# Attention scores of two heads as 64-row tiles of TensorE, units in pairs, in a transformer kernel on one core

## The reference

```python
ada = silu(c) @ W_ada + b_ada                      # shift, scale and gate of both halves
h = modulate(layernorm(x), shift_a, scale_a)
q, k, v = split(h @ W_qkv + b_qkv)                 # 16 heads of 18 channels
scores = einsum('bhqd,bhkd->bhqk', q, k) * 18 ** -0.5
o = einsum('bhqk,bhkd->bhqd', softmax(scores), v)
x = x + gate_a * (o @ W_proj + b_proj)
h = modulate(layernorm(x), shift_m, scale_m)
x = x + gate_m * (gelu(h @ W_up + b_up) @ W_down + b_down)
```

## Time and profile before

| | |
|---|---|
| median of 3 runs | 2154.39 us |
| profiled execution | 2156.56 us, span 2154.9 us |
| mean granted TensorE clock | 0.963 |
| busy, PE / weight loads | 1971.7 / 1748.4 us |
| busy, DVE / ACT / POOL | 1225.6 / 1108.3 / 1028.6 us |
| scores L1683 (768 products) | 244.2 us busy |
| shifted scores L1706 (1536 products) | 245.1 us busy |

### The profile page before, as it was taken

How to read it: one execution, slowest core, us unless ns; L and a number is a source line. 1 busy time by engine, 2 the same in 40 slices (tenths; PEclk the granted TensorE clock), 3 DMA queues, 4 the chain that set the end, 5 groups by cost and what they waited for, 6 DMA issues and landing times. The chain is left out here.

```text
span 2154.9 us, 50055 instructions
## 1 busy us (share of the span) xinstructions
PE 1971.7 (91%) x16599; PEld 1748.4 (81%) x16599; DVE 1225.6 (57%) x2813; ACT 1108.3 (51%) x1909; POOL 1028.6 (48%) x1066
## 2 busy tenths in 40 slices
PE   4684689999999999889999999989989999999996
PEld 2553479998989988778989999888779999898986
DVE  7765465565655556464655646565555556565541
ACT  2222245656465564446565564654555564646552
POOL 2002164454545545564545545445645545454544
PEclk9887689999999999999999999999999999999998
DMA  6604243333233332353333333333433333323320
GB/s 164 159 23 139 81 125 101 98 88 96 81 108 87 97 99 85 92 138 93 84 106 92 93 101 84 98 85 98 111 103 89 98 98 89 94 82 109 88 78 25
DMA packets 139389, 207.65 MB, mean 96 GB/s; under 512 B 35390, under 2 KB 95838, under 8 KB 139006
## 3 DMA queue, kind: packets, MB, share of 16 engines
q1 hardware_dynamic: 110878, 163.54, 27.6%
q10 hardware_dynamic: 24192, 27.94, 4.7%
q0 software_dynamic: 4224, 14.96, 2.4%
HBM read 99.81 MB, written 20.82 MB: 56 GB/s over the span
## 5 line engine op out<-in xcount | busy, mean ns | idle before, releaser
L1928 DVE TENSOR_REDUCE maxima<-scores 128x4 f32<-128x1024 f32 x384 | 461.3, 1224 | 188.5 <-PE scores L1683 183.8
L1259 POOL TENSOR_TENSOR hidden<-g_full,hidden 128x512 fp32r<-128x512 f32 (+1 forms) x240 | 282.4, 1186 | 326.0 <-ACT hidden L1503 325.0
L1745 PE MATMUL mlp_ps<-h_mlp,w_up 128*128 128x256 f32 (+1 forms) x3024 | 407.4, 287 | 32.4 <-ACT hidden L1503 21.0
L1745 PEld LDWEIGHTS mlp_ps<-h_mlp,w_up 128*128 128x128 f32 (+1 forms) x3024 | 376.8, 191 | 69.7 <-issue 27.9
L1460 ACT ACTIVATE probs<-scores 128x1024 f32<-128x1024 f32 x384 | 383.8, 1028 | 74.5 <-PE pv_ps L1720 45.5
L1600 PE MATMUL mlp_ps<-w_down,hidden 128*128 128x288 f32 x2592 | 391.8, 296 | 0.0
L1600 PEld LDWEIGHTS mlp_ps<-w_down,hidden 128*128 128x128 f32 x2592 | 373.2, 190 | 18.8
L1683 PE MATMUL scores<-k_stack,q_stack 108*128 108x512 f32 x768 | 244.2, 411 | 32.6 <-DMA k_stack<-qk 18.9
L1706 PE MATMUL scores<-q_stack,k_stack 110*128 110x256 f32 x1536 | 245.1, 292 | 7.8 <-DMA q_stack<-neg_max 4.6
L1706 PEld LDWEIGHTS scores<-q_stack,k_stack 110*128 110x128 f32 x1536 | 206.0, 189 | 37.4 <-issue 19.8
L1450 ACT ACTIVATE neg_max<-att_ps 16x256 fp32r<-16x256 f32 x48 | 18.0, 375 | 423.6 <-PE att_ps L1693 423.6
(11 more groups left out here) (220 smaller groups left out, 2881.4 us busy)
## 6 DMA issues: line engine op xcount, KB each, us to landing
q_stack<-qk SPq DMA_DIRECT2D x144, 180.0 KB
k_stack<-qk SPq DMA_DIRECT2D x288, 90.0 KB
inv_sum<-inv_scratch ACTq DMA_DIRECT2D x192, 128.0 KB, 2.6
k_stack<-qk SPq DMA_DIRECT2D x288, 54.0 KB
x_in<-out_x SPq DMA_DIRECT2D x48, 288.0 KB, 3.8
x_mid<-out_x SPq DMA_DIRECT2D x48, 288.0 KB, 4.1
out_x<-x_out SPq DMA_DIRECT2D x48, 288.0 KB, 3.1
q_stack<-qk SPq DMA_DIRECT2D x144, 72.0 KB
```

The source lines that it names most:

```text
L1259: tt(out, full, high.bitcast(F32), ALU.subtract).then_inc(signal, 1)
L1745: last = mm(up_bank[n % 2][:, (m % 2) * T:(m % 2 + 1) * T], w[:, m * P:(m + 1) * P], h, start=count == 0, stop=count == 6)
L1928: nc.vector.tensor_reduce(out=maxima[:, :, :, u], in_=scores[u % 2][:, :, :, :], axis=AX.X, op=ALU.max).then_inc(s_max, 1)
```

## The change

Two heads of a unit no longer share one product over 108 rows. Head 0's 54 rows lie at partitions 0 to 53 of both stacks, head 1's at 64 to 117, with the negated maxima below each (rows 54 and 118). Each product works on one half of the array's rows (`tile_position` (0, 0) or (64, 0)), and consecutive products alternate between the halves and between the two banks of a `scores` tile. A unit of unshifted scores becomes four products of 256 columns instead of two of 512; a shifted unit stays at four. The key stack loses its second axis and its zeros; it is set to ones once, which supplies the row that multiplies the maxima. Every DMA into a stack is one head's: 12 + 18 instead of 9 + 15.

Units go in pairs, `score_units` and `shifted_units`: a pair (u, u + 1) waits until both `scores` tiles are free, that is for every reader up to unit u - 1. The second group of DMAs is waited for at unit 4 instead of 5. On TensorE the new order is: query/key 0, shifted pair 0, query/key 1, pair 2, query/key 2, MLP transposes, weighted values 0, pair 4, weighted values 1, values 0, pair 6; and score pair 0 before up part 3, score pairs 2, 4, 6 before down parts 0, 2, 4. ACT's copies of the query/key parts move accordingly. Left out below: the same edits in the prologues, the row to which ACT's DMA writes, and the removal of four DVE instructions that wrote the ones.

```diff
@@ -36,7 +36,7 @@
 IN_COLS = V_START + C
 QK_USES, UP_USES = 3, 5
-PAIR_ROWS, SHIFTED_ROWS = 6 * HD, 6 * HD + 2
+HEAD_ROWS = 3 * HD
 SCALE = float(HD) ** -0.5
@@ -951,7 +951,7 @@
         qk = [sb(f"qk{i}", [QK_ROWS, QK_TILES, T], F32R) for i in range(2)]
         q_stack = sb("q_stack", [P, H // 2, T], F32R)
-        k_stack = sb("k_stack", [P, H // 2, 2, T], F32R)
+        k_stack = sb("k_stack", [P, H // 2, T], F32R)
         v_sb = sb("v_sb", [P, 2, H, 32])
@@ -1042,7 +1042,7 @@
-        PIECES_A, PIECES_B = 16 * 9, 16 * 15
+        PIECES_A, PIECES_B = 16 * 12, 16 * 18
         PRE_EXP, PRE_PV, G_PRE, PRE2, PRE = 2, 2, 2, 2, 1
@@ -1160,15 +1160,11 @@
                 hold(s_x_st, 16 * it + 16)
                 sp.dma_start(x_in[:, :, :], dram["out"][b]).then_inc(s_xin, 16)
-            def into_stack(j, part, src, rows, units, signal):
-
-                sp.dma_start(q_stack[PAIR * j:PAIR * j + PAIR, units, :].bitcast(F32),
-                             qk[part][rows, src, :].bitcast(F32)).then_inc(signal, 16)
-
-            def head_into_stack(j, par, part, src, row, units, signal, key=True):
-                dest = slice(PAIR * j + HD * par, PAIR * j + HD * par + HD)
-                stack = k_stack[dest, units, par, :] if key else q_stack[dest, units, :]
-                sp.dma_start(stack.bitcast(F32), qk[part][row:row + HD, src, :].bitcast(F32)).then_inc(signal, 16)
+            def head_into_stack(stack, j, par, part, src, row, units, signal):
+
+                first = R * par + HD * j
+                sp.dma_start(stack[first:first + HD, units, :].bitcast(F32),
+                             qk[part][row:row + HD, src, :].bitcast(F32)).then_inc(signal, 16)
             Q_PARTS, K_PARTS = (0, 1, 0), (0, 0, 1)
@@ -1178,24 +1174,21 @@
                     hold(s_st, 8 * it - 3 + PRE)
                 for j in range(3):
-                    into_stack(j, Q_PARTS[j], slice(0, 5), slice(0, PAIR), slice(0, 5), s_stack_a)
+                    for par in range(2):
+                        head_into_stack(q_stack, j, par, Q_PARTS[j], slice(0, 5), HD * par, slice(0, 5), s_stack_a)
+                        head_into_stack(k_stack, j, par, K_PARTS[j], slice(0, 5), PAIR + HD * par, slice(0, 5), s_stack_a)
+
+                hold(s_st, 8 * it + PRE)
                 for j in range(3):
                     for par in range(2):
-                        head_into_stack(j, par, K_PARTS[j], slice(0, 5), PAIR + HD * par, slice(0, 5), s_stack_a)
-
-                hold(s_st, 8 * it + PRE)
-                for j in range(3):
-                    into_stack(j, Q_PARTS[j], slice(0, 2), slice(2 * PAIR, 3 * PAIR), slice(5, 7), s_stack_b)
-                    for par in range(2):
-                        head_into_stack(j, par, Q_PARTS[j], slice(par, par + 1), 3 * PAIR, slice(7, 8), s_stack_b, key=False)
-                for j in range(3):
-                    for par in range(2):
-                        head_into_stack(j, par, K_PARTS[j], slice(2, 5), 2 * PAIR + HD * par, slice(5, 8), s_stack_b)
+                        head_into_stack(q_stack, j, par, Q_PARTS[j], slice(0, 2), 2 * PAIR + HD * par, slice(5, 7), s_stack_b)
+                        head_into_stack(q_stack, j, par, Q_PARTS[j], slice(par, par + 1), 3 * PAIR, slice(7, 8), s_stack_b)
+                        head_into_stack(k_stack, j, par, K_PARTS[j], slice(2, 5), 2 * PAIR + HD * par, slice(5, 8), s_stack_b)
             def negated_maxima(it):
                 hold(s_neg, it + 1 + PRE)
-                sp.dma_start(q_stack[PAIR_ROWS:PAIR_ROWS + 1, :, :].bitcast(F32),
+                sp.dma_start(q_stack[HEAD_ROWS:HEAD_ROWS + 1, :, :].bitcast(F32),
                              neg_max[0:H // 2, :].bitcast(F32)).then_inc(s_neg_st, 16)
...
@@ -1306,7 +1299,7 @@
                 inverse_deviation(0, 0)
                 nc.gpsimd.memset(v_sb[:, :, :, :], 1.0).then_inc(s_init, 1)
-                nc.gpsimd.memset(k_stack[:, :, :, :].bitcast(F32), 0.0).then_inc(s_kinit, 1)
+                nc.gpsimd.memset(k_stack[:, :, :].bitcast(F32), 1.0).then_inc(s_kinit, 1)
                 stage_behind(0, OF["w_in"])
...
@@ -1518,15 +1511,20 @@
                 before, after, after_next = neighbours(l, b)
                 negate_maxima(it)
-                for n in range(3):
-                    if after:
-                        qk_high(it + 1, n)
-                    if n < 2:
-                        if at(b, 1):
-                            high_weights("w_up", l, (n + 1,))
-                        exponentials(it, n)
+                if after:
+                    qk_high(it + 1, 0)
+                exponentials(it, 0)
+                if at(b, 1):
+                    high_weights("w_up", l, (1,))
+                exponentials(it, 1)
+                if after:
+                    qk_high(it + 1, 1)
                 for u in range(2, 5):
                     exponentials(it, u)
+                    if after and u == 2:
+                        qk_high(it + 1, 2)
+                    if at(b, 1) and u == 2:
+                        high_weights("w_up", l, (2,))
                     if at(b, 0) and before and u == 3:
@@ -1668,21 +1666,22 @@
                               start=count == 0, stop=count == 6)
                 last.then_inc(s_v_ps, 1)
-            def score_unit(it, u):
+            def score_units(it, u):
                 if u == 0:
                     pe.wait_ge(s_stack_a, PIECES_A * (it + 1) + 16)
-                if u == 5:
+                    pe.wait_ge(s_exp, 8 * it + PRE_EXP)
+                else:
+                    pe.wait_ge(s_max, 8 * it + u)
+                if u == 4:
                     pe.wait_ge(s_stack_b, PIECES_B * (it + 1) + 16)
-                if u < 2:
-                    pe.wait_ge(s_exp, 8 * it - 1 + u + PRE_EXP)
-                else:
-                    pe.wait_ge(s_max, 8 * it + u - 1)
-                r = slice(0, PAIR_ROWS)
-                for qt in range(2):
-                    last = mm(scores[u % 2][:, qt, :, :], q_stack[r, u, qt * P:(qt + 1) * P],
-                              k_stack[r, u, :, :], start=True, stop=True)
-                last.then_inc(s_score, 1)
+                for v in (u, u + 1):
+                    for qt in range(2):
+                        for par in range(2):
+                            r = slice(R * par, R * par + HEAD_ROWS)
+                            last = mm(scores[v % 2][:, par, qt, :], q_stack[r, v, qt * P:(qt + 1) * P],
+                                      k_stack[r, v, :], start=True, stop=True, tile_position=(R * par, 0))
+                    last.then_inc(s_score, 1)
             def maxima_transposes(it, after):
@@ -1694,18 +1693,19 @@
                                                maxima[:, qt, :, :].rearrange("p a b -> p (a b)"), ident[:, :])
                 last.then_inc(s_max_ps, 1)
-            def shifted_unit(it, u):
+            def shifted_units(it, u):
                 if u == 0:
                     pe.wait_ge(s_neg_st, 32 * it + 32 + 16)
-                if u >= 2:
-                    pe.wait_ge(s_exp, 8 * it + u - 1 + PRE_EXP)
-                r = slice(0, SHIFTED_ROWS)
-                for par in range(2):
+                else:
+                    pe.wait_ge(s_exp, 8 * it + u + PRE_EXP)
+                for v in (u, u + 1):
                     for kt in range(2):
-                        last = mm(scores[u % 2][:, par, kt, :], k_stack[r, u, par, kt * P:(kt + 1) * P],
-                                  q_stack[r, u, :], start=True, stop=True)
-                last.then_inc(s_st, 1)
+                        for par in range(2):
+                            r = slice(R * par, R * par + HEAD_ROWS + 1)
+                            last = mm(scores[v % 2][:, par, kt, :], k_stack[r, v, kt * P:(kt + 1) * P],
+                                      q_stack[r, v, :], start=True, stop=True, tile_position=(R * par, 0))
+                    last.then_inc(s_st, 1)
             def weighted_values(it, g):
...
@@ -1787,21 +1787,22 @@
                 if after and at(b, B - 1):
                     weights_ready("w_in", l + 1)
-                for n in range(3):
-                    if after:
-                        qk_tiles(it + 1, n, m_between=before)
-                    shifted_unit(it, n)
-                shifted_unit(it, 3)
+                if after:
+                    qk_tiles(it + 1, 0, m_between=before)
+                shifted_units(it, 0)
+                if after:
+                    qk_tiles(it + 1, 1, m_between=before)
+                shifted_units(it, 2)
+                if after:
+                    qk_tiles(it + 1, 2, m_between=before)
                 if before:
                     mlp_transposes(it - 1, after)
-                shifted_unit(it, 4)
                 weighted_values(it, 0)
+                shifted_units(it, 4)
                 weighted_values(it, 1)
-                shifted_unit(it, 5)
-                shifted_unit(it, 6)
                 if after:
```

(18 more changed lines are left out.)

19 lines of the change are left out of this document (5 added, 14 removed).

## The result

The changed kernel takes **2443.02 us** (median of 4 runs, 2441.1 to 2445.12), the kernel before 2153.49 beside it: ratio 1.1345, interval 1.1325 to 1.1365. Slower by 290 us; 2518 was forecast, inside 2400 to 2615. The profiled execution took 2445.12 us, span 2443.3.

The account below looks back on a forecast made before the run. PE bounds the kernel before; afterwards the loop through SP's stack copies takes 46.2 us against 37.72. 47 x 8.5 = 400, -40 at boundaries, +4 prologue: +364, giving 2518 us, range 2400 to 2615.

Parts of the forecast that it names:

- What bounds the kernel, and what takes its place: PE's own work sets the 37.72 us half-step; after the change, the wait for late stack copies at score pair 4 does.
- The loop: Shifted pair 0, stack issue, landing, score pair 4, projection, shifted pair 0: 46.2 us per half-step against 37.72.
- (a): From the first shifted product to SP's first stack issue, behind ACT's copies and exponentials and shifted unit 4: 6.96 us.
- (b): From SP's first stack issue to score pair 4's release: 30 issues at 0.785 us plus landing, 25.1 us (24.0 to 27.1).
- (c): From score pair 4 to the projection on PE: 7.1 us warm, 9.1 with the lower clock.
- (d): From the projection to the next shifted product, unchanged from the kernel before: 5.05 us.
- The drop of the clock: PE's 6.7 us idle stretch lowers the granted clock each half-step; about 5 us at half speed adds 2.0 us.
- Products side by side and changes of shape: Paired products on PE save 3.8 us per half-step; 16 more array-shape changes at 0.2 us cost 3.2; net gain 0.6.
- Layer boundaries: Of 79.5 us of PE waits at layer boundaries, half was taken to run beside the new wait: -40 us.
- The prologue: Its own stacks have six more DMAs that PE waits for, against a smaller memset and dropped writes: +4 us net.
- By the pairs and not by the DMAs: Rival: score pair 4 waits for DVE's maximum 3, 1.9 us idle, pair 6 another 0.64; 2243 us, chance 0.08.
- Faster: Rival: PE stays the bound with the new wait hidden, each half-step 0.6 us shorter; 2126 us, chance 0.04.

Follow-up runs that it names:

- e1: Kernel before with only its six wide query copies split by head, so SP issues 30 copies per half-step instead of 24; 2295.0 us, ratio 1.0638.
- e7: Changed kernel with 38 added products whose results nothing reads, in TensorE's order ahead of score pair 4; 2402.0 us, ratio 1.1147.
- e2: Kernel before with units in pairs, ACT's copies moved and the wait at unit 4; layout, products and 24 copies kept; 2403.1 us, ratio 1.1151.
- e4: Changed kernel with 9 late copies on GpSimd, DVE's normalisation behind maximum 3 and gate product of down part 2 behind maximum 5; 2199.3 us, ratio 1.0206.
- e12: As e4, but GpSimd's nine copies made once, for the first unit of work, leaving part of the computation out; 2164.2 us, ratio 1.0038.
- e3: Changed kernel with 9 of the 18 late copies issued by GpSimd, SP keeping 12 + 9; 2352.6 us, ratio 1.0926.

## Why the prediction was right

**What bounds the kernel, and what takes its place**: right. PE was the bound, without waits in an inner half-step; with the change it waits for the late copies at score pair 4, 5.44 us in the half-step shown (the stack copies are waited for 45 times between 300 and 2400). The times on the way came out too: pair 0 starts at 17.9 without a wait, as forecast, and PE is idle from 25.3, as forecast. DVE's own path to pair 4, put at 27.2, ends at 27.7, well ahead of the release at 30.8.

**The loop**, term by term, in the half-step from 471.01 to 515.55:

| term | predicted | measured | from |
|---|---|---|---|
| (a) to the first issue | 6.96 | 6.71 | 471.01 to 477.72 |
| (b) issues and landing | 25.1 | 24.08 | 477.72 to 501.80 |
| (c) pair 4 to projection | 9.1 | 8.59 | 501.80 to 510.39 |
| (d) projection to shifted product | 5.05 | 5.16 | 510.39 to 515.55 |
| sum | 46.2 | 44.5 | |

The sum is 1.7 too high, 78 us over 47, which is the miss of 75, but for a few us at the ends and the boundaries. The largest part is (b): an issue takes 0.749 us on the average of 30 (22.48 in all), not 0.785. I had let the present mean of 0.85 pull the value up; the small ones' 0.75 hold for all of them once every copy has 18 rows in one piece, the 90 KB ones too. e1 bears this out: most of its narrow query copies issue in 0.70 us, its key copies, whose rows still lie with gaps between them, mostly in 0.77. The landing, 1.60, was taken as 1.54.

In (c) the mechanism was right and the cover was missed. e7 shows 7.03 at full clock where I had 7.1, with 0.43 in it for DVE ahead of pair 6. At half clock PE's down part 2 is so slow that DVE is no longer late: no wait is shown at 507.23. I had added 2.0 for the clock to a sum that already held DVE's lateness; the two are beside each other.

**The drop of the clock**: right, once per half-step, and e7 shows its price by taking it away. The prediction rested on one wait of 5.08 us. It takes less than that: 3.11 in e2 did it, and in half of the half-steps 1.8 in e1.

**Products side by side and changes of shape**: right in mechanism, and to 0.2 to 0.4 us a half-step. A pair takes 0.67 us, predicted 0.48 and a change of 0.2, and the change splits as forecast, 0.10 behind the first products and 0.09 behind the last. The net gain was put at 0.6 us a half-step; work without waits is 36.75 in e4 (37.92 less 0.91 and 0.26, the second for exponentials at 521.09) and 36.9 in e12, so it is 0.8 to 1.0. The changed kernel agrees: 44.54 less 5.44, less a wait of 0.20 for exponentials, less 1.99 for the clock is 36.9. No run has the split copies and the new order without the row tiles, so what the row tiles do to the whole time is read from the half-steps alone.

**Layer boundaries**: -40 was forecast for waits that run beside the new one; by the intervals it is 284 - 47 x 6.8 = -36. No row stood behind the half that I took, so this is luck. The prologue was +2.1 for a forecast +4.

**The rivals.** "By the pairs and not by the DMAs" was underpriced at 2243: e3, where half of the late copies are off SP and DVE decides, takes 2353, with 2.64 us at pair 4 in an inner half-step where I had 1.9 idle, 0.44 at pair 6 and 1.22 at pair 0, and with the clock down in 14 of 33, which this rival left out. "Faster" at 2126 rested on 28 us of net gain with nothing late; no run got there, e12 being the nearest at 2164. So that rival's gain was real on TensorE and too small for what stands around it.

## What to carry to other kernels

An engine that is busy without a gap hides how little slack its suppliers have: before giving it less to do, or moving a wait forward, take the distance from the last DMA's landing to its first use (here 0.7 us) and multiply what the change adds to that queue by the cost of an issue, which here was 0.70 us for 18 KB and for 90 KB alike. A wait that returns in each period costs more than its length where the clock falls behind it (1.6 us more for 5.4 here). And when queue after queue is relieved, expect the next wait to take back most of each gain.
